# Router logits as eight more columns of two projections, in a two-layer kernel on one core

## The reference

```python
x = x + einsum('bso,ho->bsh', attn, wo)          # x here is the layernorm of the running value
h = _rmsnorm(x, ln2_w).reshape(-1, HID)          # x * rsqrt(mean(x*x) + EPS) * ln2_w
logits = einsum('th,eh->te', h, gate_w)          # 8 logits for each token
rprobs = softmax(logits, axis=-1)
topw, topi = top_k(rprobs, 2)
topw = topw / sum(topw)
for e in range(8):
    g = silu(h @ w1[e].T) * (h @ w3[e].T)
    out = out + (g @ w2[e].T) * wfull[:, e:e+1]  # wfull holds topw at topi
return x + out
```

## Time and profile before

| | before |
|---|---|
| median of 3 runs | 1739.2 us (1738.49 to 2075.5) |
| the profiled execution, by the same clock as the runs | 1730.77 us |
| its span | 1729.1 us |
| mean granted clock of TensorE | 0.968 |
| PE / PEld busy | 1624.7 us (94%) / 807.7 us (47%) |
| DVE / ACT / POOL busy | 1166.1 (67%) / 931.3 (54%) / 556.0 us (32%) |
| routing, from its first matmul to the first matmul of the experts | 1212.6 to 1345.5 us |

### The profile page before, as it was taken

The page is one execution under the profiler, slowest core; times in us unless marked ns, Lnnn a source line. Parts: engine busy times, 40 slices in busy tenths (PEclk is TensorE's granted clock), DMA queues, the critical chain, the costliest instruction groups (busy, mean ns, idle before and its releaser), DMA issues. The chain is left out here.

```text
span 1729.1 us, 29571 instructions
## 1 busy us (share of the span) xinstructions
PE 1624.7 (94%) x9040; PEld 807.7 (47%) x9040; DVE 1166.1 (67%) x3195; ACT 931.3 (54%) x2069; POOL 556.0 (32%) x842
## 2 busy tenths in 40 slices
PE   7899989899999999999999999998995899999996
PEld 3367655333333333334333343332884455565554
DVE  6722788899888888888888888870685344343342
ACT  6134544166676776676676766667573333333332
POOL 3530338163515003030030300000377344444443
PEclk9999999799999999999999999999895899999999
DMA  5000000311030300303003030000378677777774
GB/s 165 1 7 19 2 1 7 62 36 28 2 62 2 62 2 1 62 2 62 2 1 62 2 62 2 1 1 1 120 234 276 122 129 130 131 130 129 129 126 71
DMA packets 252195, 105.77 MB, mean 61 GB/s; under 512 B 208064, under 2 KB 247880, under 8 KB 252040
## 3 DMA queue, kind: packets, MB, share of 16 engines
q1 hardware_dynamic: 233296, 80.62, 22.0%
q0 software_dynamic: 13392, 18.49, 6.3%
q10 hardware_dynamic: 5352, 4.76, 0.8%
HBM read 30.88 MB, written 23.67 MB: 32 GB/s over the span
## 5 line engine op out<-in xcount | busy, mean ns | idle before, releaser
L1677 ACT ACTIVATE prob<-pS 128x512 f32<-128x512 f32 (+3 forms) x1280 | 582.3, 542 | 267.5 <-PE pS L1563 176.2
L1734 DVE TENSOR_REDUCE mx<-pM 128x1 f32<-128x512 f32 x768 | 501.6, 685 | 71.3 <-PE pM L1543 68.1
L1543 PE MATMUL pM<-KT,QT 96*128 96x512 bf16 (+3 forms) x1280 | 434.1, 356 | 16.5 <-DVE mx L1734 5.5
L1559 PE MATMUL pS<-QT,KT 99*128 99x512 bf16 (+3 forms) x1280 | 422.9, 352 | 6.8 <-ACT prob L1677 1.8
L2440 PE MATMUL bank<-w13T,QKV 128*128 x568 | 257.2, 596 | 15.4 <-ACT QKV L2467 15.4
L1730 DVE CUSTOM_DVE_ANT_0 junk<-pM,mask_row 128x128 bf16<-128x128 f32 (+3 forms) x512 | 239.9, 483 | 41.7 <-PE pM L1543 41.1
L1578 PE MATMUL pO<-prob,VV 128*32 128x512 f32 (+3 forms) x2560 | 267.8, 536 | 0.0
L1543 PEld LDWEIGHTS pM<-KT,QT 96*128 96x128 bf16 x1280 | 124.5, 98 | 208.5 <-DVE mx L1734 79.1
L1468 POOL CAST mpart<-mneg 128x16 bf16<-128x16 f32 x32 | 6.8, 213 | 653.9 <-DVE mneg L1742 653.9
L1559 PEld LDWEIGHTS pS<-QT,KT 99*128 99x128 bf16 x1280 | 123.6, 97 | 184.0 <-ACT prob L1677 140.2
L2500 DVE TENSOR_TENSOR QKV<-QKV,bank 128x512 f32<-128x512 f32 x71 | 48.8, 687 | 235.5 <-issue 200.2
(11 more groups left out here) (356 smaller groups left out, 1947.3 us busy)
## 6 DMA issues: line engine op xcount, KB each, us to landing
raw<-in_ffn_w_dram SPq DMA_DIRECT2D x48, 256.0 KB, 4.0
QKV<-queue SPq DMA_DIRECT2D x71, 136.0 KB, 2.5
out_dram<-x ACTq DMA_DIRECT2D x8, 512.0 KB, 4.7
x<-_attn_hidden_states_dram SPq DMA_DIRECT2D x14, 256.0 KB, 5.5
QKV<-QKV SPq DMA_TRANSPOSE x142, 3.2
QT<-mrow SPq DMA_DIRECT2D x128, 3.0 KB
out_dram<-QKV POOLq DMA_INDIRECT x71, 3.9
wc_s<-in_attn_Wc_dram SPq DMA_DIRECT2D x1, 1024.0 KB, 8.1
```

The costliest lines, as they stand in the source:

```text
L1543: last = nc.tensor.matmul(pM[:, bank, 0:w], QT[0:ROWS, par, h, qt * P:(qt + 1) * P], KT[0:ROWS, par, 512 * part:512 * part + w], start=Tru ...
L1559: last = nc.tensor.matmul(pS[:, p % NSC, lo:512], KT[0:ROWS + 3, par, kt * P:(kt + 1) * P], QT[0:ROWS + 3, par, h, 512 * c + lo:512 * c + ...
L1677: nc.scalar.activation(prob[:, n % RING, h, lo:512], pS[:, p % NSC, lo:512], ACT.Exp, scale=SCALE).then_inc(s.head_exp, 1)
L1734: nc.vector.reduce_max(mx[:, h, qt, part:part + 1], pM[:, plan.bank[item], 0:w], AX.X).then_inc(s.unit_max, 1)
```

## The change

The logits are linear in the sum that `attended` forms, so the change takes them from its two terms. Eight columns, the gate's weights folded into `wqkv`'s norm, are appended to `wqkvT` (392 columns); they give the part of the logits that comes from the layer's normed input, and `QKV` becomes 392 wide. Eight columns, `wo` times the gate's weights, are appended to `woT` (264 columns). `stage4` turns one weight more (`turn_weight` in seven tiles) and multiplies `wo` with `gws` (`output_gate`), one copy for each; DVE has three small operations more there. In `stage6` POOL has two operations of `[128, 32]` more, for the factor in `norm1[:, 0]`.

In routing, `turn_h`, `h_out` and `logits` are gone. A new step on POOL, `routed(q)`, scales the eight columns of a group's four tiles into `xl[:, :, 256:264]`; `attended` then waits for it and adds 264 columns, and `soften` reads the logits from `QKV`. A product of 264 columns no longer shares a bank with another, so `pX` holds three tiles (`SX` = 3), and `project` waits tile by tile. With the turned rows gone, all that follows `attended` is done one beat earlier: `LATE` is 10, and DVE's, ACT's and POOL's beats have a new order. `xl` lies in the room of `w2T` now. The two vectors with `ln2_w` are loaded elsewhere.

```diff
-            per = [0, 0, 4, 4, 4, 4, 4, 4, 8, 8, 8]
+            per = [0, 4, 4, 4, 4, 4, 4, 8, 8, 8]
...
+            def routed(q):
+                four = slice(G * q, G * q + G)
+                if q >= 1:
+                    pool.wait_ge(s.x2, G * q)
+                nc.gpsimd.tensor_tensor(xl[:, :, H:H + E], QKV[:, four, ROUTED:ROUTED + E],
+                                        v.norm1[:, 0, four].unsqueeze(2).to_broadcast([P, G, E]),
+                                        ALU.mult).then_inc(s.routed, 1)
...
             for beat in range(1, LATE):
-                if beat >= 3:
-                    scatter(beat - 3, 0, 4)
+                if beat >= 2:
+                    scatter(beat - 2, 0, 4)
+                if beat < NQ:
+                    routed(beat)
                 if beat <= NQ:
                     root2(beat - 1)
-                if beat >= 3:
-                    scatter(beat - 3, 4, 4)
+                if beat >= 2:
+                    scatter(beat - 2, 4, 4)
...
             def project(i):
                 pe.wait_ge(s.aT_out, i + 1)
-                if i >= 2:
-                    pe.wait_ge(s.x2, 2 * i - 2)
                 for j in range(2):
+                    t = 2 * i + j
+                    if t >= SX:
+                        pe.wait_ge(s.x2, t - SX + 1)
                     for c in range(C):
-                        last = nc.tensor.matmul(pX[:, 2 * (i % 2) + j, :], aT[:, i % 2, j, c, :], v.woT[:, c, :],
+                        last = nc.tensor.matmul(pX[:, t % SX, :], aT[:, i % 2, j, c, :], v.woT[:, c, :],
                                                 start=(c == 0), stop=(c == C - 1))
                     last.then_inc(s.proj, 1)
...
                 for j in range(2):
                     if beat < NQ:
                         turn_attended(2 * beat + j)
-                    if 1 <= beat <= NQ:
-                        turn_h(2 * (beat - 1) + j)
                     turn_weights(ws[j * quarter:(j + 1) * quarter])
                 for j in range(2):
                     if beat < NQ:
                         project(2 * beat + j)
-                    if 1 <= beat <= NQ:
-                        logits(2 * (beat - 1) + j)
                     if j == 0:
                         turn_weights(ws[2 * quarter:3 * quarter])
-                if beat == NQ + 1:
+                if beat == NQ:
                     total()
-                if 2 <= beat <= NQ + 1:
-                    ranks(beat - 2)
+                if 1 <= beat <= NQ:
+                    ranks(beat - 1)
                 turn_weights(ws[3 * quarter:])
...
-                for j in range(2):
-                    if beat < NQ:
-                        attended_out(2 * beat + j)
-                    if 1 <= beat <= NQ:
-                        h_out(2 * (beat - 1) + j)
-                    weights_out(ws[j * quarter:(j + 1) * quarter])
-                    if j == 0 and 2 <= beat <= NQ + 1:
-                        exponential(beat - 2)
-                    if j == 0 and beat < NQ:
-                        normal(beat)
+                if beat < NQ:
+                    attended_out(2 * beat)
+                weights_out(ws[0:quarter])
+                if beat < NQ:
+                    normal(beat)
+                    attended_out(2 * beat + 1)
+                weights_out(ws[quarter:2 * quarter])
                 if 1 <= beat <= NQ:
-                    squares(beat - 1)
+                    exponential(beat - 1)
                 weights_out(ws[2 * quarter:3 * quarter])
+                if beat < NQ:
+                    squares(beat)
...
                     dve.wait_ge(s.xl, t + 1)
-                    dve.wait_ge(s.proj, t - t % 2 + 2)
-                    nc.vector.tensor_tensor(QKV[:, t, 0:H], xl[:, t % G, :], pX[:, t % G, :], ALU.add).then_inc(s.x2, 1)
+                    dve.wait_ge(s.routed, q + 1)
+                    dve.wait_ge(s.proj, t + 1)
+                    nc.vector.tensor_tensor(QKV[:, t, 0:H + E], xl[:, t % G, :], pX[:, t % SX, :], ALU.add).then_inc(s.x2, 1)
...
-            for beat in range(LATE):
-                if 2 <= beat <= NQ + 1:
-                    soften(beat - 2)
-                    records(beat - 2)
-                    choose(beat - 2)
-                if beat == 4:
+            for beat in range(NQ + 1):
+                if beat == 3:
                     spare_out()
                 if beat < NQ:
                     attended(beat)
-                if 2 <= beat <= NQ + 1:
-                    settle(beat - 2)
-                if beat == 2:
-                    spare_hot()
+                if beat >= 1:
+                    soften(beat - 1)
+                    records(beat - 1)
+                    choose(beat - 1)
                 if beat < NQ:
                     residual(beat)
+                if beat >= 1:
+                    settle(beat - 1)
+                if beat == 1:
+                    spare_hot()
```

More of the change, by code:

```diff
@@ L44 @@
 QKVW = (NH + 2 * NKV) * HD
+ROUTED = QKVW
 E = 8
@@ L936, in turn_weight, with output_gate @@
                                                    ident[0:rows, 0:rows])
+                    last.then_inc(s.wT_mm, 1)
+                def output_gate():
+                    pe.wait_ge(s.wT_out, 6)
+                    for m in range(C):
+                        for c in range(C):
+                            last = nc.tensor.matmul(pQK[:, 1, m * E:(m + 1) * E], raw[:, 3 + c, m * P:(m + 1) * P],
+                                                    v.gws[:, c, :], start=(c == 0), stop=(c == C - 1))
                     last.then_inc(s.wT_mm, 1)
@@ L1106, in stages_layer2 @@
     with ExitStack() as late:
-        ln2_b = sb("ln2_b", [P, H], F32, late)
-        woT, gwT = v.woT, v.gwT
+        woT = v.woT
         mv5 = sb("mv5", [P, T, 2], F32, late)
@@ L1510, in project @@
                         for c in range(C):
-                            last = nc.tensor.matmul(pS[:, t % NSC, 0:QKVW], xT[:, i % 2, j, c, :], wqkvT[:, c, :],
+                            last = nc.tensor.matmul(pS[:, t % NSC, 0:QKVW + E], xT[:, i % 2, j, c, :], wqkvT[:, c, :],
                                                     start=(c == 0), stop=(c == C - 1))
@@ L1815, in stage7 @@
         turned = sb("turned7", [P, E * REC], F32, ctx)
-        aT, hT = (turned[:, 4 * C * P * n:4 * C * P * (n + 1)].rearrange("p (i j c n) -> p i j c n", i=2, j=2, c=C)
-                  for n in range(2))
+        aT = turned[:, 0:4 * C * P].rearrange("p (i j c n) -> p i j c n", i=2, j=2, c=C)
         padr = turned[:, :].rearrange("p (e w) -> p e w", e=E)
-        ln2c = sb("ln2c", [P, C], F32, ctx)
-        gws = sb("gws", [P, C, E], F32, ctx)
         raw = sb("raw8", [P, R, 512], F32, ctx)
@@ L1953, in project @@
                 pe.wait_ge(s.aT_out, i + 1)
-                if i >= 2:
-                    pe.wait_ge(s.x2, 2 * i - 2)
                 for j in range(2):
+                    t = 2 * i + j
+                    if t >= SX:
+                        pe.wait_ge(s.x2, t - SX + 1)
                     for c in range(C):
-                        last = nc.tensor.matmul(pX[:, 2 * (i % 2) + j, :], aT[:, i % 2, j, c, :], v.woT[:, c, :],
+                        last = nc.tensor.matmul(pX[:, t % SX, :], aT[:, i % 2, j, c, :], v.woT[:, c, :],
                                                 start=(c == 0), stop=(c == C - 1))
                     last.then_inc(s.proj, 1)
-            def turn_h(i):
-                pe.wait_ge(s.x2, 2 * i + 2)
-                if i >= 1:
-                    pe.wait_ge(s.hT_out, i)
-                for j in range(2):
-                    for c in range(C):
-                        last = nc.tensor.transpose(pH[:, j, c, :], QKV[:, 2 * i + j, c * P:(c + 1) * P],
-                                                   ident[:, :])
-                last.then_inc(s.hT_mm, 1)
-            def logits(i):
-                if i == 0:
-                    pe.wait_ge(s.gw_ready, C)
-                pe.wait_ge(s.hT_out, i + 1)
-                q = i // 2
-                if i % 2 == 0 and q >= 1:
-                    pe.wait_ge(s.soft, 2 * (q - 1) + 1)
-                if i % 2 == 0 and q >= 2:
-                    pe.wait_ge(s.place, q - 1)
-                for j in range(2):
-                    for c in range(C):
-                        last = nc.tensor.matmul(logits_at[:, 2 * (i % 2) + j, :], hT[:, i % 2, j, c, :], gws[:, c, :],
-                                                start=(c == 0), stop=(c == C - 1))
-                last.then_inc(s.logits, 1)
             def ranks(q):
@@ L2124, in route_act @@
                 weights_out(ws[3 * quarter:])
-                if 2 <= beat <= NQ + 1:
-                    q = beat - 2
+                if 1 <= beat <= NQ:
+                    q = beat - 1
                     act.wait_ge(s.resid, q + 1)
@@ L2150, in soften @@
                 dve.wait_ge(s.rstd2, q + 1)
-                dve.wait_ge(s.logits, 2 * q + 2)
```

(3 more changed lines are left out.)

107 lines of the change are left out of this document (58 added, 49 removed).

## The result

The changed kernel takes 1774.6 us (median; 1771.3 to 1775.3) and the kernel before 1738.9 us. The ratio is 1.0205, with a 95% interval of 1.019 to 1.022: slower by 35.7 us, some 2%. One of the four executions of the kernel before took 2075.5 us, the other three lie within 0.7 us of each other. The profiled execution of the changed kernel took 1774.3 us, like its others; the one of before was 8 us shorter than the median of its own.

The account below looks back on a forecast made before the run. DVE and POOL hand-overs, no full engine, pace routing before; afterwards they close a ring. 35 + 4 + 0.5 - 2 + 0.5 = +38 us: 1777 us from the median 1739.2, range 1762 to 1790.

Parts of the forecast that it names:

- The ring: Routing: DVE waits for `routed` behind four POOL transfers needing DVE's row numbers; 16.8 us a turn for 11.6, +35 in all.
- Last interval: Routing, seventh to eighth group's row numbers: no `attended` or `residual`, but the root behind four transfers; 15.0 us.
- The named signs: Routing: DVE idle some 6 us before L2138, L2219 near 17 us apart, POOL idle before L1942, PE's clock under 0.86.
- The clock term: Routing's middle: TensorE partly at 1.2 GHz makes the fourth tile and turns with eight weights or spare tokens late; +4 (0 to 10).
- Work removed at nothing: Routing: the turnings and logits taken off PE and copies off ACT gain nothing, as DVE and POOL pace the beat.
- The beginning: Routing up to the first group's row numbers: less PE work but perhaps half clock; +0.5 us (-2 to +4).
- The tail: End of routing: records land earlier, ACT's padding rows become last; -2 us, or -7 if weight loads come faster.
- Before routing: `stage4` and `stage6`: one more weight turned, wider matmuls, small DVE and POOL operations; +0.5 us (0 to 3).
- at full clock PE is in time: Routing: TensorE has 6.7 us of work behind `ranks`, and the ring leaves it some 10.
- no ring: Rival, routing: DVE finds `routed` done, POOL's own queue paces; -6 us, 1733 us, not slower; chance 0.08.
- a shorter ring: Rival, routing: POOL starts in 0.3 us, clock stays up, tail gives 7; +24 us, 1763 us; chance 0.18.
- The upper end of the term: Routing: TensorE falls to half clock every turn, the clock term is 10 and the sum some 6 us higher.

Follow-up runs that it names:

- eight_transfers: Changed kernel with all eight POOL transfers, in place of four, ahead of `routed` and the root; 1810.0 us, ratio 1.0434.
- ranks_later: Changed kernel with the `ranks` matmuls on TensorE a beat later, behind the beat's first pair of `project`, POOL's order unchanged; 1780.2 us, ratio 1.0262.
- warm: Changed kernel with ten unused matmuls added on TensorE ahead of `ranks` in beats 1 to 7; 1769.5 us, ratio 1.0203.
- before_light: Kernel before, in its old order, with most of the turnings, copies and logits matmuls that the change removes taken out; 1736.7 us, ratio 0.9994.
- both_first: Changed kernel with `routed` and the root both ahead of all eight transfers in POOL's beat; 1763.6 us, ratio 1.0156.
- pool_open_warm: both_first with ten unused matmuls added on TensorE ahead of `ranks` in beats 1 to 7; 1755.2 us, ratio 1.0107.

## Why the prediction was right, step by step

**The ring.** The mechanism is the one named, and eight_transfers and the last intervals show it by dose. Term by term, forecast and then measured in the turn from 1299.77 to 1316.51 us: POOL starts 0.9, 0.81; four transfers with `routed`'s wake-up 4.8, 4.77; `routed` with its hand-over 0.35, 0.46; `attended` 2.0, 2.12; `soften` to `choose` 6.6, 6.54; `residual` 1.2, 1.14; `settle` 0.9, 0.90. Sum 16.8, measured 16.7. Last interval 15.0, measured 14.9. The named signs are there: 6.03 us ahead of L2138 by L1931 (so in four of the six turns; in the first it is 3.7 us, behind 2.6 us of work on the spare tokens, in the second DVE waits for others), POOL idle ahead of L1942 by L2219, TensorE's clock at 0.74. The wait for L1994, named as a sign of being wrong, is there with 0.67 us, but it is the fourth tile's, which `attended` has in its 2.0.

**The clock term, +4.** The size holds: six turns of 16.7 and one of 14.9 are 115.3, measured 118.7, so 3.4 us more. They lie in three turns (17.2, 18.6, 17.8), two of which are those where the prediction had TensorE late: the one with the spare tokens, where DVE waits 2.2 us for their matmuls and then 4.2 us for `normal`, and the one with eight weights. The fourth tile at half clock, the other half of the term, did not occur in the changed kernel (0.67 us of wait); it showed in eight_transfers, ranks_later and two turns of `warm` (1.64). Of the 3.4 us, 1.9 are the clock's by `warm`, in the turn with the spare tokens. The turn with eight weights is only 0.3 us shorter there; TensorE waits in it for loads too. So the term was right in size, and one trace shows the clock as the cause of 1.9 us of it. The cause of the rest is open.

**Work removed at nothing.** Right: before_light.

**The beginning, +0.5.** From routing's start to the first row numbers 24.45 us, 0.2 more than in the earlier trace rows.

**The tail, -2.** The padding rows are last, as forecast, but the tail shrank by 3.9. ACT issued its last one 14.3 us behind the eighth row numbers (forecast 15.0) and it took 1.73 us to land, not the 2.44 of a record; from landing to the experts 8.0 us. Mis-sized, within -2 to -7.

**Before routing, +0.5.** Not contradicted; the spread of the executions hides it.

The sum by the traces: against the first profile of before, 10.2 + 0.2 + 37.7 - 3.9 = 44 us; against the second, whose ring is 83.4, the ring's part is 35.3. The medians say 35.7, forecast 38. The 2% at which the prediction divides slower from the same, 34.8 us, lies inside the interval of the ratio (1.019 to 1.022), so on which side of it the change falls is not decided. The experts take 382.8 us, 383.6 before: no part of it.

**Where the working was weak.** The step "at full clock PE is in time", 6.7 us of work against some 10, looked at what fits into a turn, not at what waits for what. It missed that `ranks`, waiting, holds the next group's projections, a ring of 15.0 us just below that of 16.7. The forecast was not hurt, since the longer ring sets the pace. But the rival "no ring" was too rosy: its condition was only that POOL's ring does not close, and it gave 1733. That was done in both_first, by the order of POOL's queue: 1763.6. The rival "a shorter ring", 24 us slower than before, has this time but not this reason.

The rule cited from the Trainium skill, "TensorE: Matmul & The Clock Gate", section "HAM oscillation — how this bites in real kernels", holds in part: the clock does fall in every turn, behind each wait of 6 us, and recovers within it. The upper end of the term, to which the rule led, did not come: what the fall costs hangs on which ring TensorE is in, 8.4 us in its own, 1.9 us of one turn in POOL's.

The other one from the Trainium skill, "Perfetto Trace Analysis", section "Identifying the Most-Contended Engine", was applied in the prediction to TensorE's matmul time, 70.2 us. The section itself calls that time no good measure of how close TensorE is to its limit and takes its weight loads; by these, 62.9 us, TensorE was level with DVE's 63.8. Taking work off the engine with the most busy time gave nothing, as forecast (before_light).

## What to carry to other kernels

When a change removes a beat of distance between producer and consumer, write down for each in-order queue what stands behind every waiting instruction, and follow it round until it closes; each such ring has a length, and the time follows the longest. Opening the longest gains only down to the next, here 1.7 us a turn, so two edits can be worth far more together than each alone: here 11 us and a loss of 6, together 35. And a profile where two engines each idle in turn, one released by the other, with no engine full, shows a ring; an engine's busy share doesn't.

## What was not expected of the hardware

- TensorE's clock in a turn: behind a wait of 6.15 us four turnings took 1.06 to 1.12 us for about 5 us, then 0.60 us again. In pool_open_warm a wait of 1.76 us ahead of `ranks` was also followed by turnings of 1.09 and 1.06 us, as one of 1.58 us was by half clock in the earlier trace rows. A wait of 1.79 us one turn earlier was not: the turnings behind it took 0.60 to 0.65 us. So the length of the last wait alone doesn't tell which clock follows.
- Work whose result nobody used made a kernel 8.4 us faster, by keeping the clock at 0.88 in place of 0.72.
- Executions of the same early code enter routing up to 10 us apart (1212.5 to 1222.8 us), and TensorE's clock differs in layer 1, whose code the change doesn't touch: 0.97 between 50 and 100 us in the first profile of before, 0.89 in the changed kernel's. One profile of each kernel would have put 10 us to the change that are not its own.
